# A convolution with pyramid attention on one core: the last batch's scores moved to the start of their steps, six output banks, x of second tiles in halves, and one low part made by VectorE

## The chip, the cores and the metric

The program runs on one NeuronCore of a Trainium2 chip. The metric is the device time of a whole execution in microseconds (us), the median of several runs. Before the change it is 1314.9 us, the median of 3 runs (1314.38 to 1315.77).

The engines named below: PE (TensorE, the matmuls), DVE (VectorE), ACT (ScalarE), POOL (GpSimd) and SP (SyncE, which issues nearly all DMAs). SBUF is the memory on the core, PSUM the eight banks of 128 x 512 numbers that the matmuls write.

## The reference

The input `x` has 8 images of 512 channels with 64 x 64 points. What is computed for each image:

```python
qk = relu(bn(conv1x1(x, qk_w)))            # 256 channels
val = relu(bn(conv1x1(x, v_w)))            # 512 channels
key = psp(qk)                              # max over 1, 9, 36 and 64 windows: 110 cells
value = psp(val).transpose(0, 2, 1)        # 110 cells
query = qk.reshape(B, Ck, H * W).transpose(0, 2, 1)
scores = softmax(einsum('bnc,bcs->bns', query, key) * Ck ** (-0.5))
y = einsum('bns,bsc->bnc', scores, value).transpose(0, 2, 1).reshape(B, Cv, H, W)
return x + bn(conv1x1(y, out_w))
```

All is float32. Keys and values of an image are known only when the whole image has been convolved, so the attention of an image is worked on while the next one is convolved.

## The kernel before, in words

An image is cut into 8 tiles of 512 points; there are 64 tiles (`S`). Every float32 operand of a matmul is split into a high part (`xh`, `wh`, ..: a copy in the fp32r format) and a low part (`xl`, `wl`, ..: the number less its high part), and each product is made of three matmuls of 128 x 128 by 128 x 512 (high x high, low weights x high, high x low), which add up in a PSUM bank. ACT makes the high parts of x, POOL the low parts.

The order of the instructions on each engine is written out by hand; engines wait for each other by counting semaphores. There are three stages.

- Steps 0 and 1 convolve a tile each with plain products. Then come 27 **pairs** (`s` = 1 to 27) of two tiles each. A pair uses a scheme with 7 products in place of 8 (`pair_product`, three times a pair: j = 0, 1, 2; each product part is 6 matmuls, so a j has 42). It needs 7 parts of x (`PARTS`): four blocks of the raw x of the two tiles (B11, B21 of the first, B12, B22 of the second; in `xa`) and three sums of them (`tt[0]` to `tt[2]`, and T3, which overwrites B12), made by POOL in `sums_of_x` (4 instructions). ACT makes the high part of each (`split_part_hi`, L964), then POOL the low part (`split_part_lo`, L578), in the order 0 to 6. With j = 0 PE takes the parts in the same order and waits for the low part of each (`x_ready`). Between its products PE does the attention of tiles 8 behind (`scores`, `sums`, `project`), from pair 4 on.
- DVE pools: row maxima of each product's bank (`pool_pair_rows(s, j, r)`, L1336), cells from the rows (`pool_cells`), and at an image's end the grids. It also adds `u5` in two places (`make_u4` L1399, `make_u7` L1405; PE waits for both), and does steps of the softmax and the final add. In pair 4, 8, 12, .. an image has ended (`batch_ended`), and DVE makes the key cells and grids ahead of `make_u4`.
- SP loads x for pair s + 1 during the lows of pair s: tile 2s + 2 once parts 0 to 3 are split, tile 2s + 3 once part 5 is (`load`, two DMAs of 512 KB each).
- **Steps** 56 to 63 (`LAST` to `S` - 1) convolve the queries' and keys' channels of the last image, tile by tile; steps 64 to 71 (`S` to `X` - 1) load x again and convolve its value channels (`conv(s, 0..3)`, 12 matmuls each), with the softmax of the last image's tiles 56 to 62 beside it: `sums(a)` (2 matmuls) of the tile before at the start of a step, `scores(a)` (6 matmuls) in its middle. The chain for a tile a is: scores on PE, `exps` on ACT (two instructions), `split_e_lo` on DVE, `sums` on PE, `guess` on ACT (two), `refine` (two) and `normalise` on DVE, `split_p_hi` on ACT, `split_p_lo` on DVE; after that `project(a, m)` may run. The queries of tile a are split by `split_q_hi` (ACT) and `split_q_lo` (POOL).
- The **tail**: when the last value cells are there, PE projects all eight tiles 56 to 63 of the last image (`project(a, m)`, m = 0 to 3, 3 matmuls each, 96 in all, and the `sums` of tiles 62 and 63 among them). The output banks are four in turn (`out_bank`), one for each m. DVE adds m = 0, 2, 3 to x (`add_out`, L1476), ACT copies m = 1 out of its bank (`copy_out`, L1235) and POOL adds it (`add_copy`, L608); SP stores each half tile of 512 KB.

## Time and profile before

| | us |
|---|---|
| median of 3 runs | 1314.9 (1314.38 to 1315.77) |
| the profiled execution | 1314.11 |
| its span in the profile | 1312.4 |
| PE busy in the span | 1283.3 (98%) |
| DVE busy | 947.3 (72%) |
| ACT busy | 688.7 (52%) |
| POOL busy | 951.9 (73%) |

The span is what the trace covers; the profiled execution took 1.7 us more than that. A time is read as a start in us from the span's start, then a duration. Where PE is busy 98% of the span, its few idle microseconds are what a change of order can win, and they are in two places: up to about 170 us, and after 1272 us.

### The profile page before, as it was taken

To read this page: it belongs to the slowest core of one execution; us is meant where nothing else is said; L and a number is where in the kernel's file an instruction comes from. 1 tells how busy PE (TensorE), PEld (TensorE's weight loads), DVE (VectorE), ACT (ScalarE), POOL (GpSimd) and SP (SyncE) were. 2 spreads that over 40 slices of the span, in tenths; PEclk is the share of its full clock that TensorE was granted. 3 is DMA by queue.
4 is the path that set the end of the run, shared out by engine and by line. 5 is a ranking of instruction groups with operands and counts; after the bars stand their busy time and mean duration, and the time that the engine had idled before them with its cause. 6 is when DMAs were issued, how large, how long until landed. Compare 5 with 4: busy or idle time off the path is not lost.

```text
span 1312.4 us, 16789 instructions
## 1 busy us (share of the span) xinstructions
PE 1283.3 (98%) x5539; PEld 1036.1 (79%) x5539; DVE 947.3 (72%) x2171; ACT 688.7 (52%) x1017; POOL 951.9 (73%) x414
## 2 busy tenths in 40 slices
PE   7999999999999999999999999999999999999996
PEld 6777788887888878887888877888788887888875
DVE  6555677777777778778777777777867778876466
ACT  5333555644555654555654465654555647754421
POOL 1888988877878867887777786877778826765522
PEclk9999999999999999999999999999999999999998
DMA  6323356566676656676556676666667669995226
GB/s 225 113 97 113 112 177 213 196 217 223 210 240 217 198 187 232 211 238 224 182 207 232 222 232 204 205 200 233 206 219 239 211 205 365 331 308 201 96 97 257
DMA packets 134538, 272.20 MB, mean 207 GB/s; under 512 B 9227, under 2 KB 9267, under 8 KB 134451
## 3 DMA queue, kind: packets, MB, share of 16 engines
q1 hardware_dynamic: 133874, 270.07, 60.9%
q10 hardware_dynamic: 576, 1.05, 0.2%
q8 instruction: 45, 0.74, 0.2%
q14 instruction: 43, 0.34, 0.1%
HBM read 174.61 MB, written 96.47 MB: 207 GB/s over the span
## 4 chain that ended last, share of the span: by engine, by line
PE 79%; DVE 7%; POOL 7%; ACT 3%; DMA 2%; issue 2%; SPq 0%; DVEq 0%; ACTq 0%; POOLq 0%
PE conv_ps L690 16%; PE conv_ps L688 16%; PE conv_ps L692 16%; POOL xl L578 5%; PE out_ps L772 4%; PE out_ps L773 3%; PE out_ps L774 3%; PE conv_ps L673 3%; PE conv_ps L674 3%; PE conv_ps L672 3%; PE score_ps L746 2%; PE score_ps L745 2%; PE score_ps L747 2%; DVE row_max L1336 1%; DMA xa<-x 1%
## 5 line engine op out<-in xcount | busy, mean ns | idle before, releaser
L1336 DVE TENSOR_REDUCE row_max<-conv_ps 128x64 f32<-128x384 f32 (+2 forms) x576 | 284.5, 530 | 149.0 <-ACT q_out L1035 68.2
L578 POOL TENSOR_TENSOR xl<-xa,xh 128x1024 fp32r<-128x1024 f32 x108 | 258.0, 2418 | 84.5 <-ACT xh L964 84.5
L688 PE MATMUL conv_ps<-xh,sh 128*128 128x512 f32 x648 | 253.5, 391 | 3.8 <-POOL xl L578 1.8
L690 PE MATMUL conv_ps<-xh,sl 128*128 128x512 f32 x648 | 254.3, 393 | 0.0
L692 PE MATMUL conv_ps<-xl,sh 128*128 128x512 f32 x648 | 254.3, 392 | 0.0
L578 POOL TENSOR_TENSOR xl<-tt,xh 128x1024 fp32r<-128x1024 f32 x81 | 194.3, 2415 | 10.2 <-ACT xh L964 10.2
L688 PE MATMUL conv_ps<-xh,wh 128*128 128x512 f32 x486 | 190.2, 391 | 4.1 <-POOL xl L578 2.7
L692 PE MATMUL conv_ps<-xl,wh 128*128 128x512 f32 x486 | 190.7, 392 | 0.0
L690 PE MATMUL conv_ps<-xh,wl 128*128 128x512 f32 x486 | 190.6, 392 | 0.0
L972 ACT ACTIVATE conv_ps<-conv_ps 128x512 f32<-128x512 f32 x81 | 47.2, 583 | 253.6 <-PE conv_ps L692 252.9
L1476 DVE SCALAR_TENSOR_TENSOR xo<-out_ps,shift,xo 128x512 f32<-128x512 f32 x205 | 151.9, 745 | 34.5 <-DMA xo<-x 18.0
L602 POOL TENSOR_TENSOR q_l<-q_in,q_h 128x1024 fp32r<-128x1024 f32 x50 | 120.7, 2415 | 47.5 <-ACT q_h L1041 47.5
L688 PEld LDWEIGHTS conv_ps<-xh,sh 128*128 128x128 f32 x648 | 121.7, 188 | 35.7 <-POOL xl L578 4.2
L690 PEld LDWEIGHTS conv_ps<-xh,sl 128*128 128x128 f32 x648 | 121.6, 188 | 28.0
L692 PEld LDWEIGHTS conv_ps<-xl,sh 128*128 128x128 f32 x648 | 121.6, 188 | 26.1
L572 POOL TENSOR_TENSOR xl<-xa,xh 128x1024 fp32r<-128x1024 f32 x34 | 81.4, 2405 | 58.6 <-ACT xh L949 58.6
L589 POOL TENSOR_TENSOR tt<-xa 128x1024 f32<-128x1024 f32 x27 | 64.9, 2405 | 78.0 <-DMA xa<-x 78.0
L688 PEld LDWEIGHTS conv_ps<-xh,wh 128*128 128x128 f32 x486 | 91.3, 188 | 29.2 <-POOL xl L578 4.4
L964 ACT ACTIVATE xh<-xa 128x1024 fp32r<-128x1024 f32 x108 | 113.5, 1055 | 1.4
L690 PEld LDWEIGHTS conv_ps<-xh,wl 128*128 128x128 f32 x486 | 91.2, 188 | 20.6
L692 PEld LDWEIGHTS conv_ps<-xl,wh 128*128 128x128 f32 x486 | 91.2, 188 | 19.4
L672 PE MATMUL conv_ps<-xh,wh 128*128 128x512 f32 x240 | 94.9, 395 | 0.0
(227 smaller groups left out, 2527.7 us busy)
## 6 DMA issues: line engine op xcount, KB each, us to landing
xa<-x SPq DMA_DIRECT2D x148, 512.0 KB, 5.5
xo<-x SPq DMA_DIRECT2D x104, 512.0 KB, 4.3
out<-xo SPq DMA_DIRECT2D x104, 512.0 KB, 3.7
queries<-q_out SPq DMA_DIRECT2D x112, 256.0 KB, 2.5
...
```

What stands on the lines that cost most here:

```text
L572: nc.gpsimd.tensor_tensor(xl[:, b:b + 2, :], xa[:, part, s % 2, :, :], xh[:, b:b + 2, :], ALU.subtract)\
L578: nc.gpsimd.tensor_tensor(xl[:, b0:b1, :], raw, xh[:, b0:b1, :], ALU.subtract).then_inc(x_lo, 1)
L589: nc.gpsimd.tensor_tensor(T1, B12, B11, ALU.subtract).then_inc(t_made, 1)
L602: nc.gpsimd.tensor_tensor(q_l[:, :, :], q_from(a), q_h[:, :, :], ALU.subtract).then_inc(q_lo, 1)
L672: nc.tensor.matmul(bank(s, c)[:, :], wh[:, k, cols], hi, start=(k == 0), stop=False)
L688: nc.tensor.matmul(out[:, :], hi[:, k, :], xh[:, b + k, :], start=first, stop=False, skip_group_check=True)
L690: nc.tensor.matmul(out[:, :], lo[:, k, :], xh[:, b + k, :], start=False, stop=False, skip_group_check=True)
L692: last = nc.tensor.matmul(out[:, :], hi[:, k, :], xl[:, b + k, :], start=False, stop=end, skip_group_check=True)
L772: nc.tensor.matmul(bk[:, :], vo_h[:, cols], hi, start=True, stop=False)
L964: nc.scalar.activation(xh[:, b0:b1, :], raw, ACT.Copy).then_inc(x_hi, 1)
L1336: last = nc.vector.tensor_reduce(row_max[:, c, n, :], src[:, r0_ * W:r1_ * W].rearrange("p (r w) -> p w r", w=W), AX.X, ALU.max)
L1476: nc.vector.scalar_tensor_tensor(xt, out_bank(a, m)[:, :], shift[:, CC + m:CC + m + 1], xt, ALU.add, ALU.add)\
```

## The change

Four edits of order and none of arithmetic:

1. In pairs 2 to 4 (`BY_VECTOR`) the low part of part 5 (B22, `VECTOR_PART`) is made by DVE and no more by POOL. It stands in DVE's program between the third and the fourth row pooling of the pair before with j = 2. Who waited for `x_lo` now waits for `x_lo` and, where needed, `x_lo_vector` (`wait_lo`).
2. SP loads B12 of the second tile of the next pair after part 4 and B22 after part 5; before, both after part 5. POOL's first sum waits for the first half alone (`wait_x_half`).
3. In steps 65 to 70 `scores(a)` stands at the start of the step and `sums(a)` of the same tile in its middle (before: `sums` of the tile before at the start, `scores` in the middle), so that tile 62's softmax ends in step 70 and leaves the tail. ACT, DVE and POOL have their parts of the chain moved to match.
4. The tail turns through six banks (`LAST_BANKS`) and waits for the add (or the copy) of the block six before; `project(56, m)` for m = 1 to 3 waits for no add. `sums(63)` follows tile 57's blocks, not tile 58's.

```diff
@@ parts
+        BY_VECTOR, VECTOR_PART = (2, 3, 4), 5
+        def wait_lo(eng, s, n):
+            v = vector_parts(s)
+            if s in BY_VECTOR and n > VECTOR_PART:
+                v += 1
+            wait(eng, x_lo_vector, v)
+            eng.wait_ge(x_lo, x_parts(s) + n - v)
...
+        LAST_BANKS = [out_ps[0], *conv_ps[0:3], out_ps[1], score_ps]
         def out_bank(a, m):
-            return [out_ps[0], *conv_ps[0:3]][m] if a >= LAST else out_ps[m % 2]
+            return LAST_BANKS[(OC * (a - LAST) + m) % len(LAST_BANKS)] if a >= LAST else out_ps[m % 2]
@@ sync
-                sp.wait_ge(x_lo, x_parts(s) + 6)
-                load(2 * s + 3)
+                wait_lo(sp, s, 5)
+                load_half(2 * s + 3, 0)
+                wait_lo(sp, s, 6)
+                load_half(2 * s + 3, 1)
@@ gpsimd
-                for t in range(2):
-                    wait_x(pool, 2 * s + t)
+                wait_x(pool, 2 * s)
+                wait_x_half(pool, 2 * s + 1, 0)
                 nc.gpsimd.tensor_tensor(T1, B12, B11, ALU.subtract).then_inc(t_made, 1)
                 pool.wait_ge(t_made, 4 * (s - 1) + 1)
+                wait_x_half(pool, 2 * s + 1, 1)
...
                 for i in range(OPS):
-                    split_part_lo(s, i)
+                    if not by_vector(s, i):
+                        split_part_lo(s, i)
...
-                if LAST < s < S:
+                if s < X - 1 and s not in (LAST, S):
                     split_q_lo(s - (NT - 1))
@@ tensor: project
+                n = OC * (a - LAST) + m
+                if n >= len(LAST_BANKS):
+                    n -= len(LAST_BANKS)
+                    if copied(LAST + n // OC, n % OC):
+                        pe.wait_ge(y_copied, n // OC + 1)
+                    else:
+                        pe.wait_ge(out_added, added(LAST + n // OC, n % OC))
...
@@ tensor: steps 64 to 71
-                if s < X - 1:
+                if s <= S + 1:
                     sums(ap)
...
+                elif s < X - 1:
+                    scores(ac)
                 conv(s, 0)
                 conv(s, 1)
...
                 elif s < X - 1:
-                    scores(ac)
+                    sums(ac)
                 conv(s, 2)
...
-            sums(S - 2)
...
-                if a == LAST + 2:
+                if a == LAST + 1:
                     sums(S - 1)
@@ scalar: steps 65 to 70
+            for s in range(S + 1, X - 1):
+                a = s - NT
+                if s == S + 1:
+                    guess(a - 1)
+                exps(a)
+                split_q_hi(a + 1)
+                split_hi(s + 1, 0)
+                split_hi(s + 1, 1)
+                if s == S + 1:
+                    split_p_hi(a - 1)
+                guess(a)
+                split_p_hi(a)
@@ vector
+            def split_vector_part_lo(s):
+                raw, b0, b1 = PARTS[VECTOR_PART]
+                dve.wait_ge(x_hi, part_number(s, VECTOR_PART))
+                nc.vector.tensor_tensor(xl[:, b0:b1, :], raw, xh[:, b0:b1, :], ALU.subtract).then_inc(x_lo_vector, 1)
...
                 pool_pair_rows(s, 2, 2)
+                if s + 1 in BY_VECTOR:
+                    split_vector_part_lo(s + 1)
                 pool_pair_rows(s, 2, 3)
...
             split_e_lo(S - 1)
-            refine(S - 2)
             add_outs(LAST + 1)
-            normalise(S - 2)
             add_outs(LAST + 2)
-            split_p_lo(S - 2)
+            refine(S - 1)
             add_outs(LAST + 3)
-            refine(S - 1)
             normalise(S - 1)
```

The order on DVE from behind `make_u7` of pair 3, j = 2, to `make_u4` of pair 4, before (a row maximum is `row_max`, `make_u4` is L1399; `cells`, `part` and `rows` are the key cells and grids of the image that has ended):

```order
L1336 TENSOR_REDUCE row_max<-conv_ps 128x64 x4
L1379 TENSOR_REDUCE cells<-row_max 128x2x8
L1384 TENSOR_REDUCE part<-row_max 128x2x2 x6
L1377 TENSOR_REDUCE cells<-row_max 128x2x8
L1384 TENSOR_REDUCE part<-row_max 128x2x2 x3
L1419 TENSOR_REDUCE cells<-part 128x2x36
L1421 TENSOR_REDUCE rows<-cells 128x36
L1423 TENSOR_REDUCE cells<-rows 128x2x9
L1425 TENSOR_REDUCE cells<-cells 128x2
L1399 TENSOR_TENSOR conv_ps<-conv_ps,u 128x512
```

and with the change (the same operations have the lines 1397, 1460, 1438 to 1445 and 1480 to 1486):

```order
L1397 TENSOR_REDUCE row_max<-conv_ps 128x64 x2
L1511 TENSOR_TENSOR xl<-xa,xh 128x1024
L1397 TENSOR_REDUCE row_max<-conv_ps 128x64 x2
L1440 TENSOR_REDUCE cells<-row_max 128x2x8
L1445 TENSOR_REDUCE part<-row_max 128x2x2 x6
L1438 TENSOR_REDUCE cells<-row_max 128x2x8
L1445 TENSOR_REDUCE part<-row_max 128x2x2 x3
L1480 TENSOR_REDUCE cells<-part 128x2x36
L1482 TENSOR_REDUCE rows<-cells 128x36
L1484 TENSOR_REDUCE cells<-rows 128x2x9
L1486 TENSOR_REDUCE cells<-cells 128x2
L1460 TENSOR_TENSOR conv_ps<-conv_ps,u 128x512
```

The new subtraction `xl<-xa,xh` stands ahead of the last two row maxima, and so ahead of the chain of cells and grids that ends in `make_u4`.

The order on PE in the tail, tiles 56 and 57 (`e_h`, `sh`: exponentials of the tiles, `vo`: the projected values; three rows are one block), before:

```order
L772 MATMUL out_ps0<-sh,vo_h 128x512 [waits rows_pooled,out_added,vo_lo,p_lo]
...
L772 MATMUL conv_ps0<-sh,vo_h 128x512 [waits out_added,rows_pooled,vo_lo]
...
L772 MATMUL conv_ps1<-sh,vo_h 128x512 [waits out_added,rows_pooled,vo_lo]
...
L772 MATMUL conv_ps2<-sh,vo_h 128x512 [waits out_added,rows_pooled,vo_lo]
...
L772 MATMUL out_ps0<-e_h,vo_h 128x512 [waits out_added,p_lo]
...
L772 MATMUL conv_ps0<-e_h,vo_h 128x512 [waits y_copied]
```

and with the change:

```order
L826 MATMUL out_ps0<-sh,vo_h 128x512 [waits rows_pooled,out_added,vo_lo,p_lo]
...
L826 MATMUL conv_ps0<-sh,vo_h 128x512 [waits rows_pooled,vo_lo]
...
L826 MATMUL conv_ps1<-sh,vo_h 128x512 [waits rows_pooled,vo_lo]
...
L826 MATMUL conv_ps2<-sh,vo_h 128x512 [waits rows_pooled,vo_lo]
...
L826 MATMUL out_ps1<-e_h,vo_h 128x512 [waits p_lo]
...
L826 MATMUL score_ps<-e_h,vo_h 128x512 [waits p_lo]
```

The fifth and the sixth block go to `out_ps1` and `score_ps` and wait for no add; the waits for an add in the first tile are gone but for one at its first block.

The order on PE at the start of step 65, before: the two `sums` of tile 56, then the first rows of `conv(65, 0)`.

```order
L755 MATMUL sum_ps<-sh,ones 128x512 [waits rsum_ready,e_lo]
L756 MATMUL sum_ps<-sl,ones 128x512
L672 MATMUL conv_ps2<-xh,wh 128x512 [waits x_lo,rows_pooled]
L673 MATMUL conv_ps2<-xh,wl 128x512
L674 MATMUL conv_ps2<-xl,wh 128x512
```

With the change, the `scores` of tile 57 stand between them:

```order
L798 MATMUL sum_ps<-sh,ones 128x512 [waits rsum_ready,e_lo]
L799 MATMUL sum_ps<-sl,ones 128x512
L788 MATMUL conv_ps3<-q_h,key_h 128x512 [waits p_lo,q_lo]
L789 MATMUL conv_ps3<-q_h,key_l 128x512
L790 MATMUL conv_ps3<-q_l,key_h 128x512
L788 MATMUL conv_ps3<-q_h,key_h 128x512
L789 MATMUL conv_ps3<-q_h,key_l 128x512
L790 MATMUL conv_ps3<-q_l,key_h 128x512
L715 MATMUL conv_ps2<-xh,wh 128x512 [waits x_lo,x_lo_vector,rows_pooled]
```

They wait for `q_lo`, which POOL makes at the end of step 64.

## Rows read from the trace of the kernel before

**Rows 1.** Windows: us; busy of PE, PEld, DVE, ACT, POOL; PE clock; DMA; GB/s.

```profile
42.00:170.00 128.00, 121.56 (x518) 95.80 (x517) 73.94 (x185) 53.78 (x80) 110.36 (x48) 1.00 0.33 111
...
1272.00:1312.40 40.40, 27.91 (x106) 20.17 (x104) 24.73 (x41) 9.82 (x16) 8.97 (x7) 0.90 0.56 208
```

**Rows 2.** Timeline of PE, pairs 2 to 4: start, duration, [idle before <- releaser].

```profile
86.14 0.39 PE L688 MATMUL conv_ps<-xh,sh 128*128 128x512 f32 x1
...
87.27 0.39 PE L692 MATMUL conv_ps<-xl,sh 128*128 128x512 f32 x1
88.24 0.50 PE L688 MATMUL conv_ps<-xh,sh 128*128 128x512 f32 x1 [0.58 <-POOL xl L578]
...
90.57 0.50 PE L688 MATMUL conv_ps<-xh,wh 128*128 128x512 f32 x1 [0.66 <-POOL xl L578]
...
121.67 0.50 PE L688 MATMUL conv_ps<-xh,wh 128*128 128x512 f32 x1 [0.68 <-POOL xl L578]
...
148.81 0.47 PE L688 MATMUL conv_ps<-xh,sh 128*128 128x512 f32 x1 [0.64 <-DVE conv_ps L1399]
...
152.46 0.50 PE L688 MATMUL conv_ps<-xh,wh 128*128 128x512 f32 x1 [0.65 <-POOL xl L578]
```

**Rows 3.** Timeline of POOL, low parts 3 to 5 of pairs 2 and 4; first sum of pair 3.

```profile
81.08 7.10 POOL L578 TENSOR_TENSOR xl<-xa,xh 128x1024 fp32r<-128x1024 f32 x3
...
95.42 2.40 POOL L589 TENSOR_TENSOR tt<-xa 128x1024 f32<-128x1024 f32 x1 [4.90 <-DMA xa<-x]
...
142.95 7.12 POOL L578 TENSOR_TENSOR xl<-xa,xh 128x1024 fp32r<-128x1024 f32 x3
```

**Rows 4.** Timeline of DVE, ends of pairs 1 and 3.

```profile
81.17 0.69 DVE L1336 TENSOR_REDUCE row_max<-conv_ps 128x64 f32<-128x512 f32 x1 [0.83 <-ACT q_out L1035]
...
144.56 0.82 DVE L1336 TENSOR_REDUCE row_max<-conv_ps 128x64 f32<-128x384 f32 x2 [0.83 <-ACT q_out L1035]
...
147.96 0.70 DVE L1399 TENSOR_TENSOR conv_ps<-conv_ps,u 128x512 f32<-128x512 f32 x1
```

**Rows 5.** Timeline: POOL and DVE at 160 us.

```profile
159.29 2.40 POOL L591 TENSOR_TENSOR tt<-xa,tt 128x1024 f32<-128x1024 f32 x1
161.65 2.79 POOL L592 TENSOR_TENSOR xa<-xa 128x1024 f32<-128x1024 f32 x1
...
160.24 1.93 DVE L1438 TENSOR_TENSOR value_l<-cells,value_h 128x440 fp32r<-128x440 f32 x1
```

**Rows 6.** By source line: count, shortest/median/longest in ns.

```profile
L1438 DVE TENSOR_TENSOR value_l<-cells,value_h x7: 606/608/1929, 160.2 to 1090.8; 128x440 fp32r<-128x440 f32 x7
L1433 DVE TENSOR_TENSOR key_l<-key_d,key_h x8: 378/1536/2407, 154.8 to 1173.2; 128x220 fp32r<-128x220 f32 x8
L1282 DVE TENSOR_TENSOR xl<-xa,xh x2: 1225/1226/1226, 7.0 to 9.8; 128x1024 fp32r<-128x1024 f32 x2
```

**Rows 7.** Timeline, step 64 to 65: PE and POOL.

```profile
1181.49 0.39 PE L756 MATMUL sum_ps<-sl,ones 128*128 128x512 f32 x1
...
1179.55 2.40 POOL L602 TENSOR_TENSOR q_l<-spare_h,q_h 128x1024 fp32r<-128x1024 f32 x1 [2.98 <-ACT q_h L1041]
```

**Rows 8.** Timeline of PE in the tail.

```profile
1274.77 0.47 PE L772 MATMUL out_ps<-sh,vo_h 128*128 128x512 f32 x1 [0.59 <-issue]
...
1286.17 0.50 PE L772 MATMUL conv_ps<-e_h,vo_h 128*128 128x512 f32 x1 [2.10 <-ACT row_max L1235]
...
1297.34 0.40 PE L773 MATMUL out_ps<-sh,vo_l 128*128 128x512 f32 x1
...
1305.30 0.40 PE L774 MATMUL conv_ps<-sl,vo_h 128*128 128x512 f32 x1
```

**Rows 9.** Timeline of DVE and windows (columns as in group 1), tail.

```profile
1304.36 2.15 DVE L1476 SCALAR_TENSOR_TENSOR xa<-conv_ps,shift,xa 128x512 f32<-128x512 f32 x3
...
1287.50:1290.00 2.50, 2.50 (x7) 1.95 (x6) 1.24 (x2) 0.36 (x1) 1.32 (x2) 0.50 0.55 210
...
1307.50:1310.00 2.50, 0.00 (x0) 0.00 (x0) 0.00 (x0) 0.00 (x0) 0.00 (x0) 0.55 1.03 381
```

More of the change, by code:

```diff
@@ L138, in psp_attention @@
         out_ps = [psum(f"out_ps{i}") for i in range(2)]
-        x_in = [sem(f"x_in{i}") for i in range(2)]
+        x_in = sem("x_in")
+        x_in_odd = [sem(f"x_in_odd{i}") for i in range(2)]
         xo_in = [sem(f"xo_in{i}") for i in range(4)]
@@ L281, in pair_banks, with vector_parts, by_vector @@
             return conv_ps[0], conv_ps[2 - n % 2], conv_ps[1 + n % 2], conv_ps[3]
+        BY_VECTOR, VECTOR_PART = (2, 3, 4), 5
+        def vector_parts(s):
+            return len([p for p in BY_VECTOR if p < min(s, PAIRS)])
+        def by_vector(s, i):
+            return s in BY_VECTOR and i == VECTOR_PART
         def part_number(s, i):
@@ L420, in tile_of, with load_half @@
                 return v[i // NT, :, :, i % NT * TN:(i % NT + 1) * TN]
+            def load_half(s, i):
+                sp.dma_start(xa[:, i, s % 2, :, :], tile_of(x_v, tile_at(s))[:, 2 * i:2 * i + 2, :])\
+                    .then_inc(x_in_odd[i] if s % 2 else x_in, 16)
             def load(s):
-                for i in range(2):
-                    sp.dma_start(xa[:, i, s % 2, :, :], tile_of(x_v, tile_at(s))[:, 2 * i:2 * i + 2, :])\
-                        .then_inc(x_in[s % 2], 16)
+                load_half(s, 0)
+                load_half(s, 1)
             def load_residual(h):
@@ L541, in _ @@
                     for a in (LAST + 5, LAST + 7):
-                        sp.wait_ge(x_lo, x_parts(X) - (2 if a == LAST + 5 else 0))
+                        wait_lo(sp, X, -2 if a == LAST + 5 else 0)
                         load_residuals(a)
@@ L634, in _ @@
                         split_lo(n, 1)
-                if s < X - 1 and not LAST < s < S:
+                if s in (LAST, S):
                     split_q_lo(s - (NT - 1))
@@ L938, in split_hi @@
                 if s == 0:
-                    act.wait_ge([x_first, x_in[0]][part], 16)
+                    act.wait_ge([x_first, x_in][part], 16)
                 else:
@@ L1184, in _ @@
                 store_pair_q(s, 3)
-            for s in range(LAST, X):
+            for s in range(LAST, S + 1):
                 ap, ac = s - NT - 1, s - NT
-                if 0 <= ap < S - 2:
-                    guess(ap)
+                guess(ap)
                 if s == LAST + 1:
@@ L1222, in _ @@
                     continue
-                if 0 <= ac < S - 1 and not LAST < s < S:
+                if s == S:
                     exps(ac)
-                if 0 <= ac + 1 < S and not LAST < s < S:
                     split_q_hi(ac + 1)
@@ L1668, in _ @@
                 for c in range(VC):
+                    if c == 2 and S < s < X - 1:
+                        refine(ac)
+                        normalise(ac)
                     pool_tile_rows(s, c)
+                    if c == 2 and S < s < X - 1:
+                        split_p_lo(ac)
                     if s == X - 1:
@@ L1676, in _ @@
                         add_out(ap, 2 * c - 1)
-                    if c == 2 and s < X - 1:
+                    if c == 2 and s == S:
                         split_e_lo(ac)
```

52 lines of the change are left out of this document (31 added, 21 removed).

## The prediction, as put on record before the kernel was run

> **What bounds the kernel now.** I read the page's busy shares first. PE is busy 1283.3 us of 1312.4, so a change of order can win only from the 29.1 us in which PE idles, or from matmuls at a lower clock. The windows by stage come next: 42 to 170 us hold 6.4 us of PE idleness (128.00 less 121.56), and from 1272 us to the end 12.5 us (40.40 less 27.91) [rows 1]; most of the rest lies in the setup before 42 us, which the change leaves alone. In the stretch between, PE has work, so that a wait removed or added on DVE, ACT or POOL costs nothing there unless PE meets it. Third, PE's timeline, where each stop names its releaser: in pairs 2 and 3 it stops twice each for a low part from POOL, in pair 4 once for `make_u4` on DVE and once for POOL [rows 2]. In the tail it stops for adds and for a copy [rows 8].
>
> A stop costs more than its idle time. From 87.27 to 88.24 us two matmuls start 0.97 apart where the usual distance is 0.23 (86.14 and 87.27 are five apart), so an idle time of 0.58 costs 0.74 [rows 2]. I add 0.16 to each idle time.
>
> **Part 1: DVE makes a low part in pairs 2 to 4.** Without anything else it looks like this. POOL makes seven low parts back to back, one each 2.36 us: 81.08 is part 3, and three take 7.10 [rows 3]. PE catches up with part 5 (88.24) and part 6 (90.57). If DVE makes part 5, part 6 is ready 2.36 sooner, and both stops go: 0.74 + 0.82 in pair 2, and 0.84 twice in pair 3 (both its stops have idle 0.68, of which one row stands) [rows 2]. The same subtraction takes DVE 1.23 us in the setup, where POOL is idle [rows 6].
>
> But in the pairs POOL isn't idle, and the trace shows what such an instruction meets. At 160.24 us DVE starts `value_l<-cells,value_h`, with two inputs in SBUF, while POOL is in a subtraction that began at 159.29. The DVE instruction takes 1.93 in place of 0.61, and ends at 162.17; POOL's next one, started at 161.65, takes 2.79 in place of 2.40 [rows 5, 6]. So DVE waited until POOL's instruction was over, then ran, and POOL's next waited for it. `key_l<-key_d,key_h` shows the same: 0.38 at best, 2.41 at worst, never more than one POOL instruction of wait [rows 6]. The new subtraction has two inputs in SBUF as well (`xa`, `xh`).
>
> The Trainium skill states this as a rule, in "SBUF — State Buffer", section "Who interferes with whom": a DVE instruction with two SBUF inputs contends with a GpSimd instruction that reads SBUF, and the one that comes later blocks for the whole instruction. By that rule the new part is no free gain; the trace agrees, with 1.93 against 0.61.
>
> Now the sum with the lock. In pair 2 DVE is free after the third row pooling at 81.86 (81.17 + 0.69) [rows 4]. POOL is in part 3 until 83.44 (81.08 + 2.36). So DVE waits 1.58, runs until 84.67, and the record should show some 2.8 us. POOL's part 4 ends later by nearly DVE's time: at 161.7 DVE ran 0.48 (161.69 to 162.17) and POOL's next took 0.39 longer, 0.1 less than that [rows 5], so 1.23 - 0.1 = 1.13. Part 4 then ends at 86.93 in place of 85.80. PE wanted it at 86.14 [rows 2] and stops 0.8 to 0.85, with the 0.16 a cost of 0.95. After that part 5 is long there, and part 6 (89.3) is ready before PE, now at 89.8 or later. Pair 2: 0.95 in place of 1.56, a gain of 0.6. Pair 3 the same way: 0.95 in place of 1.68, a gain of 0.7.
>
> Pair 4 goes the other way. DVE is free at 143.73 (144.56 less the idle 0.83), POOL's part 3 lasts until 145.31 (142.95 + 2.36), DVE's new instruction until 146.54, and the last row maxima start at 146.55, not at 144.56 [rows 3, 4]. What follows on DVE up to `make_u4` is a chain without a gap (144.56 to 147.96: maxima, cells, grids), so `make_u4` is 2.0 us later, and it is what PE stops for at 148.81 [rows 2, 4]. This stop grows from 0.80 to 2.8. The stop for part 6 (0.81) goes, as PE comes later. Net a loss of 1.2. In pairs 2 and 3 `make_u4` doesn't suffer: DVE is done with the maxima around 85.4, and PE is at part 4 until then waiting for POOL anyway.
>
> Part 1 in all: -0.6 - 0.7 + 1.2 = -0.1, with bounds -3.6 (no lock: -1.56 - 1.68, in pair 4 -0.8 and +0.4 for 1.23 us of DVE in place of a 0.83 gap) and +1.5 (each of DVE's waits a full 2.4).
>
> **Part 2: x in halves.** The first sum of pair 3 waits 4.90 for the DMA [rows 3]. With the halves the load of B12 goes out after part 4 (86.9, against 88.2) and the sum no longer waits for the second half, 512 KB or 1.4 us at the 381 GB/s of [rows 9]: the sum starts about 2.5 us sooner. Nothing on PE waits for that sum now: POOL's low part 0 starts when ACT's high part 0 is there, and that follows PE. Cost and gain nothing from pair 5 on; in pairs 3 and 4 it is what lets POOL keep up with a PE that comes 0.6 to 1.3 sooner, so I give it no term of its own. SP's other loads and stores stand behind the same wait as before.
>
> **Part 3: scores at the step's start.** The matmuls are the same, 56 in a step. What must hold is that q's low part is ready when the step begins. At the first such step it isn't quite: POOL ends it at 1181.95 (1179.55 + 2.40), while PE would start tile 57's scores at 1181.72 (1181.49 + 0.23) [rows 7]. One stop of 0.3 with the 0.16 on top: +0.4, bounds 0 and 1. In later steps q's low part is made in the first half of the step before. POOL has 7.2 us of work in a step of 12.8 us, DVE some 8; ACT comes to x's high parts after exp, copy and q (2.3 us behind the scores), and the low parts then end about 11 us into the step, 1.8 us before the next step asks for them at the earliest. No term.
>
> **Part 4: the tail.** PE's first block starts at 1274.77, behind the value projection, which the change leaves where it is. From there to the last matmul at 1305.30 there are 98 matmuls [rows 8]. Without a stop one follows another at 0.234 (1297.34 to 1305.30 are 34 distances), so the last would start at 1274.77 + 0.08 (the first takes 0.47, not 0.39) + 97 x 0.234 = 1297.55, 7.75 sooner. That includes matmuls at half clock: in 1287.5 to 1290 the granted clock is 0.50, the 1.2 GHz level, behind the stop of 2.10 before 1286.17 [rows 8, 9]; without stops PE should stay at 2.4 GHz.
>
> Is PE free of stops? With six banks a block waits for the add six blocks (4.2 us) back. I walked DVE's new list: 25 adds at 0.70 (three took 2.15 [rows 9]), and five softmax instructions of tile 63, 3.1 together: 20.6 us from the first output at 1275.8, so DVE would be done at 1296.4 if it never waited for PE. Its lag behind PE is greatest at tile 59 (the two `refine` stand before its adds), about 1.4 us, and six banks cover 4.2. Tile 63's own chain ends (low part) near 1291.2, and PE wants it at 1294.9. What four banks and tile 62's `refine`, `normalise` and low part cost is gone. What is late next is the store. The DMA queues move 381 GB/s at the end [rows 9]: 1.05 MB of a tile in 2.75, and PE makes a tile in 12 x 0.234 = 2.81. So the stores just keep up, and the 5.9 us from the last add (1306.51) to the end stay. Tail: -7.7, bounds -7.8 and -4.5 (DMA at 330 GB/s over the eight tiles would give back 3).
>
> **Sum.** -0.1 + 0.4 - 7.7 = -7.4. The profiled execution took 1314.11, 1.7 more than its span, and would take 1306.7; the median of the runs is 0.8 above it, so I say 1307.5.
>
> **The rivals.**
> A, no lock: DVE slips in between, the new instruction takes 1.23, and part 1 gives -3.6. For it: the setup row with 1.23. Against it: 1.93 and 2.41 under the same conditions. 1314.9 - 3.6 + 0.4 - 7.7 = 1304.0.
> B, the tail is handed to the next limit: stores fall behind or DVE's lag reaches the banks, and PE stops again, about 3 us given back. For it: the DMA's share is 1.03 at the end already [rows 9]. That gives 1307.5 + 3 = 1310.5.
> C, the tail gives little, some 2 us in place of 7.7, and the time is 1313: the adds were the limit, and six banks only move the stop. Against it: DVE's 20.6 us of work under PE's 22.8.
> D, slower: POOL in steps 65 to 70 has q's low part first, and x's low parts end after the next step's first matmuls want them. The margin is 1.8 us in 12.8. A step late by 3 us in all would stop PE six times at 1.2 to 2 us; from 1.25 a step on the tail's gain is eaten, at 2.0 a step the time is 1314.9 + 12 - 7.4 = 1319.5. Against it: the walk under part 3, which finds 11 us for a chain that may take 12.8.
> That the change doesn't do what it says, I exclude: the order shows every moved instruction.
>
> **Chances.** Forecast 0.60, A 0.15, B 0.15, C 0.06, D 0.04. A difference under 0.2% (2.6 us) can't be told from none. Faster: the forecast, A, B, 0.91 with a little of C; same 0.05; slower 0.04. The forecast alone reaches from 1306 to 1309; with A and most of B the range is 1303.6 to 1310.6.
>
> **What would show it.** DVE's three new subtractions at about 2.8 us each (right) or 1.2 (A); POOL's part 4 in pairs 2 to 4 at 3.5 in place of 2.4; one stop of PE in pairs 2 and 3, at part 4, and one of about 2.6 idle in pair 4 behind `make_u4`; a stop of 0.3 before tile 57's scores; no stop of PE in the tail and no clock under 1.0 before its last matmul, which starts 7 to 8 us sooner than before, 30.5 less 7.7 = 22.8 us behind the first. Wrong would be new stops at the starts of steps 66 to 71 (D), or `out_ps` and `conv_ps` blocks of the tail waiting for DVE (B, C).

## The result, and the profile after

| | before | after |
|---|---|---|
| median | 1315.13 (1314.38 to 1315.77, 4 runs) | 1306.38 (1304.19 to 1307.34, 4 runs) |
| profiled execution / span | 1314.11 / 1312.4 | 1305.49 / 1303.8 |
| PE busy | 1283.3 | 1280.0 |
| DVE busy | 947.3 | 959.3 |

The ratio is 0.9932 (95% interval 0.9916 to 0.9948, that is 6.8 to 11.0 us less). The forecast was 1307.5, its range 1303.6 to 1310.6.

The two stretches where PE idled, beside [rows 1]; columns as there.

```profile
42.00:170.00 128.00, 121.14 (x515) 96.73 (x514) 83.94 (x187) 53.76 (x80) 106.42 (x44) 0.99 0.34 115
1270.00:1303.80 33.80, 26.81 (x114) 20.76 (x112) 23.77 (x46) 8.12 (x13) 9.09 (x7) 0.98 0.67 249
1275.00:1297.50 22.50, 22.50 (x97) 18.21 (x98) 19.45 (x32) 7.03 (x11) 9.09 (x7) 1.00 0.76 283
```

The tail's 22.5 us are full, at a granted clock of 1.00. The pairs are not better: PE's busy time there is 121.14 where it was 121.56, DVE's is up by 10 us (73.94 to 83.94), and the clock reads 0.99.

**The tail.** PE's timeline of the changed kernel: the end of the value projection and the first block, and the last matmul.

```profile
1273.46 0.39 PE L843 MATMUL out_ps<-woT_h,value_l 128*128 128x512 f32 x1
1274.91 0.47 PE L826 MATMUL out_ps<-sh,vo_h 128*128 128x512 f32 x1 [1.06 <-issue]
...
1297.57 0.40 PE L828 MATMUL conv_ps<-sl,vo_h 128*128 128x512 f32 x1
```

From first to last it is 22.66 us, without a stop, where it was 30.53 [rows 8]: 7.87 less. Two of the stops that are gone stood in tile 56, the tail's first. There the kernel before let block m wait for the add of the block ahead, although each had a bank of its own (PE before):

```profile
1276.72 0.47 PE L772 MATMUL conv_ps<-sh,vo_h 128*128 128x512 f32 x1 [0.31 <-DVE xo L1476]
...
1278.67 0.47 PE L772 MATMUL conv_ps<-sh,vo_h 128*128 128x512 f32 x1 [1.01 <-DVE xo L1476]
```

The longest stop, 2.10 before 1286.17 [rows 8], waits for ACT's copy, and the copy stands in ACT's program behind tile 62's high part, which waited 7.76 us for the last step of that tile's softmax on DVE (ACT before):

```profile
1284.95 0.60 ACT L1095 ACTIVATE sh<-score_ps 128x512 fp32r<-128x512 f32 x1 [7.76 <-DVE score_ps L1459]
1285.44 0.68 ACT L1235 ACTIVATE row_max<-conv_ps,shift 128x512 f32<-128x512 f32 x1
```

**Pairs 2 and 4.** The same view: where pair 2 had two stops [rows 2], there is one, at part 4. Pair 4's stop behind `make_u4` is 2.46, and the matmuls behind it start some 0.42 apart in place of 0.23. The last row is the window of that piece, with the clock at 0.50, the 1.2 GHz level.

```profile
85.61 0.39 PE L735 MATMUL conv_ps<-xl,wh 128*128 128x512 f32 x1
86.61 0.50 PE L731 MATMUL conv_ps<-xh,sh 128*128 128x512 f32 x1 [0.61 <-POOL xl L616]
...
145.20 0.39 PE L735 MATMUL conv_ps<-xl,wh 128*128 128x512 f32 x1
148.05 0.47 PE L731 MATMUL conv_ps<-xh,sh 128*128 128x512 f32 x1 [2.46 <-DVE conv_ps L1460]
...
150.06 0.63 PE L731 MATMUL conv_ps<-xh,sh 128*128 128x512 f32 x1
150.48 0.63 PE L733 MATMUL conv_ps<-xh,sl 128*128 128x512 f32 x1
```
```profile
149.70:152.20 2.50, 2.50 (x8) 1.92 (x7) 1.52 (x3) 0.00 (x0) 2.50 (x2) 0.50 0.52 188
```

DVE's new instruction over the whole program, by line, and its timeline and POOL's in pair 2 (before: [rows 3, 4]):

```profile
L1511 DVE TENSOR_TENSOR xl<-xa,xh x3: 2665/2790/2790, 81.5 to 141.1; 128x1024 fp32r<-128x1024 f32 x3
```
```profile
81.52 2.79 DVE L1511 TENSOR_TENSOR xl<-xa,xh 128x1024 fp32r<-128x1024 f32 x1
84.23 0.81 DVE L1397 TENSOR_REDUCE row_max<-conv_ps 128x64 f32<-128x384 f32 x2
```
```profile
80.81 5.75 POOL L616 TENSOR_TENSOR xl<-xa,xh 128x1024 fp32r<-128x1024 f32 x2
```

POOL's two parts take 5.75 where three took 7.10 [rows 3], two thus 4.73: part 4 is 1.0 longer, with DVE's turn in it.

**Pair 1, which I had not looked at.** The halves bring POOL's first sum of pair 2 from 63.42 to 58.70, and there it meets DVE's split of the weight combinations, `sl`, which also has two SBUF inputs. DVE before, then DVE, POOL and PE after:

```profile
61.24 1.22 DVE L1311 TENSOR_TENSOR sl<-s_raw,sh 128x1024 fp32r<-128x1024 f32 x1
62.37 1.22 DVE L1311 TENSOR_TENSOR sl<-q_in,sh 128x1024 fp32r<-128x1024 f32 x1
```
```profile
60.21 1.95 DVE L1372 TENSOR_TENSOR sl<-s_raw,sh 128x1024 fp32r<-128x1024 f32 x1
62.09 3.41 DVE L1372 TENSOR_TENSOR sl<-q_in,sh 128x1024 fp32r<-128x1024 f32 x1
```
```profile
58.70 2.39 POOL L627 TENSOR_TENSOR tt<-xa 128x1024 f32<-128x1024 f32 x1 [0.98 <-DMA xa<-x]
61.16 3.25 POOL L630 TENSOR_TENSOR tt<-xa,tt 128x1024 f32<-128x1024 f32 x1
64.38 3.37 POOL L631 TENSOR_TENSOR xa<-xa 128x1024 f32<-128x1024 f32 x1
```
```profile
62.22 0.50 PE L731 MATMUL conv_ps<-xh,sh 128*128 128x512 f32 x1 [1.43 <-DVE sl L1372]
```

PE's stop for `sl` was 0.68 before. It follows the first of the two records: first records of 1.22, 1.95, 2.13, 2.46 and 3.17 us (before, this trace, and runs 1, 3 and 8 below) have stops of 0.68, 1.43, 1.60, 1.93 and 2.64 behind them. A long second record alone cost nothing at this stop: in run 6, which has no part 2, it is 3.42 and the stop 0.69.

### The profile page after: what moved, and what is told of

Read it like the earlier page. It is cut to its first block, busy times and chain, and to the rows that moved or that the text cites. A ratio compares the mean times of both kernels' runs of the same rounds, so it can differ in the third digit from the quotient of the medians.

```text
span 1303.8 us, 16985 instructions
## 1 busy us (share of the span) xinstructions
PE 1280.0 (98%) x5539; PEld 1036.2 (79%) x5539; DVE 959.3 (74%) x2174; ACT 689.2 (53%) x1017; POOL 949.7 (73%) x411
## 4 chain that ended last, share of the span: by engine, by line
PE 85%; DVE 7%; ACT 3%; POOL 3%; issue 2%; DMA 0%; DVEq 0%; SPq 0%; ACTq 0%
PE conv_ps L733 17%; PE conv_ps L731 17%; PE conv_ps L735 17%; PE out_ps L826 4%; PE out_ps L827 4%; PE conv_ps L716 4%; PE conv_ps L715 4%; PE conv_ps L717 4%; PE out_ps L828 4%; POOL xl L616 3%; PE score_ps L789 2%; PE score_ps L788 2%; PE score_ps L790 2%; DVE row_max L1397 1%; ACT xh L1019 1%
## 5 line engine op out<-in xcount | busy, mean ns | idle before, releaser
L616 POOL TENSOR_TENSOR xl<-xa,xh 128x1024 fp32r<-128x1024 f32 x105 | 253.8, 2437 | 95.7 <-ACT xh L1019 95.7
L610 POOL TENSOR_TENSOR xl<-xa,xh 128x1024 fp32r<-128x1024 f32 x34 | 81.1, 2405 | 35.0 <-ACT xh L1004 35.0
```

The costliest lines, as they stand in the source:

```text
L610: nc.gpsimd.tensor_tensor(xl[:, b:b + 2, :], xa[:, part, s % 2, :, :], xh[:, b:b + 2, :], ALU.subtract)\
L616: nc.gpsimd.tensor_tensor(xl[:, b0:b1, :], raw, xh[:, b0:b1, :], ALU.subtract).then_inc(x_lo, 1)
```

## The experiments

The kernel before was timed beside each group of runs on the same chip (medians 1313.97 to 1315.07), so ratios carry the comparison; a median is set beside another only where the two ran together. Intervals of the ratios are about 0.0013 to each side (1.7 us). "Extra" below is start to start less the usual distance, idle time plus 0.16.

Effects of 1 us are small against such intervals, but PE runs the same matmuls in the same order through the pairs, so each profiled execution can be held against the trace of before at the same matmul. The table has how much later (+) or sooner (-) than before three matmuls start, those at 60.07, 85.00 and 170.01 us in the trace of before: the first number is the difference that is there at 60 us, the others are what is added to it in the stretch with pair 1's `sl` and in pairs 2 to 4.

| kernel | at 60 us | 60 to 85 us | 85 to 170 us |
|---|---|---|---|
| changed | -1.03 | +0.74 | +0.13, half clock in pair 4 |
| run 1, the same again | +0.26 | +0.91 | -1.04 |
| run 5, changed up to the tail | -0.16 | +0.91 | -1.10 |
| run 7, no halves | +0.03 | -0.02 | +0.20, half clock |
| run 11, POOL's sum waits for `sl` | +0.60 | 0.00 | +0.19, half clock |
| run 2, no part 1 | -0.80 | -0.02 | -0.11 |
| run 12, no parts 1 and 2 | +1.20 | -0.03 | -0.34 |
| run 6, before with five banks | +0.55 | -0.02 | +1.23 |
| run 3, pairs 2 and 3 | 0.00 | +1.21 | -2.20 |
| run 8, pairs 2 and 3, late load | -0.63 | +3.51 | -2.16 |
| run 9, pairs 2 and 3, sum waits | -0.70 | -0.02 | -2.13 |
| run 10, part 0 | -0.17 | -0.02 | -2.85 |
| run 4, one input from PSUM | +0.13 | +1.12 | -4.76 |

The first column is scatter for the most part: of the change only the load for pair 2 acts before 60 us, and run 12, without that, has the largest number there. Run 6 has the pairs of before and still loses 1.23 in them, to three stops for low parts in pair 4 (0.66, 0.68 and 0.68) where before has two stops in all, and one for `make_u7` (0.49): so a single trace can be off by that much. The three kernels with pairs 2 and 3 agree within 0.07.

**1. The changed kernel once more.** No edit.

> The changed kernel as it is, timed once more as the yardstick of the runs beside it. Both theories: about 1306.4 us, ratio to before 0.993. Its first four times lay 3.1 us apart (1304.19 to 1307.34), those of before 1.4. If the clock's fall behind make_u4 in pair 4 (8 matmuls at half clock, 1.5 us) comes in only some executions, the spread returns and the best times lie near 1305; if it comes always, this profile shows it again at the same place.

Measured: 1306.22 (1305.64 to 1307.03), ratio 0.9933. Pair 4's stop is there again (idle 2.42), but the clock behind it stays at 1.00:

```profile
149.70:152.20 2.50, 2.50 (x12) 2.03 (x13) 1.24 (x3) 1.07 (x4) 2.50 (x2) 1.00 1.03 397
```

So the half clock (1.5 us) comes in some executions. Run 5's trace, which has the same pairs, is the second without it, behind the same idle time of 2.42:

```profile
149.70:152.20 2.50, 2.50 (x13) 2.05 (x12) 1.44 (x3) 0.61 (x2) 2.50 (x2) 1.00 0.95 361
```

In pair 1 `sl` stopped PE for 1.60.

**2. Without part 1.**

```diff
-        BY_VECTOR, VECTOR_PART = (2, 3, 4), 5
+        BY_VECTOR, VECTOR_PART = (), 5
```

> The changed kernel without part 1: POOL makes all seven low parts again. Theory 'lock': DVE's subtraction waits for POOL and POOL for it, so part 1 gives nothing in sum. The changed kernel stops 0.77 in pair 2, 0.81 in pair 3, 2.62 in pair 4 and loses 1.53 at half clock behind that, 5.7 in all; without part 1 the stops should be those of before, 1.56 + 1.68 + 1.6 = 4.8. So this kernel is 0.9 us FASTER than the changed one, about 1305.5. Rival 'DVE's help is worth its cost': this kernel is slower by 3 us or more, 1309.5, as the forecast's case A had it.

Measured: 1306.60 (1305.31 to 1308.56), ratio 0.9936 (0.9923 to 0.9949). The stops of before are back (extras 0.75, 0.85, 0.74, 0.84, 0.80, 0.81). The time is that of the changed kernel within the scatter, and the rival with 3 us is out. The medians can't tell the 0.9 us that I expected. By the table, pairs 2 to 4 add -0.11 here and -0.34 in run 12, against about +0.2 with part 1 where the half clock comes and -1.1 where it doesn't: part 1 loses some 0.4 or gains some 0.9.

**3. DVE's part in pairs 2 and 3 alone.**

```diff
-        BY_VECTOR, VECTOR_PART = (2, 3, 4), 5
+        BY_VECTOR, VECTOR_PART = (2, 3), 5
```

> The changed kernel with DVE's low part in pairs 2 and 3 alone. Theory 'lock, and make_u4 behind it': pairs 2 and 3 keep their single stops of about 0.8 (gain 0.8 each), pair 4 goes back to two stops of about 0.8 and no half clock, so 4.15 - 1.6 = 2.5 us less than the changed kernel, about 1303.9. Rival 'the loss in pair 4 is only moved': what PE gains there it loses again at the next stop (values or scores of tile 0), and the time stays within 0.5 us of 1306.4.

Measured: 1305.18 (1304.35 to 1306.33), ratio 0.9924 (0.9911 to 0.9936), 1.0 below run 1. Pair 4 is back at extras of 0.82 and 0.82, as expected, but PE's stop for `sl` in pair 1 was 1.93 here. By the table the loss in pair 4 is 2.3 where the half clock comes (-2.20 for +0.13; 2.5 was expected) and 1.2 where it doesn't (for -1.04 in run 1), and the rival, that what is gained there is lost again at the next stop, is not borne out up to 170 us. Against runs 2 and 12 the two pairs gain some 1.9.

**4. The same subtraction with one input from PSUM.** The values of that low part are then not x's.

```diff
-                nc.vector.tensor_tensor(xl[:, b0:b1, :], raw, xh[:, b0:b1, :], ALU.subtract).then_inc(x_lo_vector, 1)
+                nc.vector.tensor_tensor(xl[:, b0, :], sum_ps[:, :], xh[:, b0, :], ALU.subtract)
+                nc.vector.tensor_tensor(xl[:, b0 + 1, :], sum_ps[:, :], xh[:, b0 + 1, :], ALU.subtract)\
+                    .then_inc(x_lo_vector, 1)
```

> The changed kernel, but DVE's low part is made by two 512-wide subtractions that take the first input from a PSUM bank in place of x in SBUF (the values of this part are then not x's low part; size, place and waits are the same). Theory 'lock': with one SBUF input nothing is shared with POOL, so each takes some 0.6 to 0.7 us in the record with no wait in it, 1.3 in sum in place of 2.8, and POOL's part 4 takes 2.4 in place of 3.5. The stops of pairs 2 and 3 (0.77, 0.81) go, that of make_u4 in pair 4 falls from 2.46 idle to about 1.3, and the half clock behind it goes: 1.6 + 1.3 + 1.5 = some 4.3 us less, about 1302. Rival 'the subtraction is slow in the pairs for another reason (its operands in SBUF are being written, or DMA traffic)': the xh input and the output are still there, the record keeps 2 us or more, and the time stays near 1306.

Measured: 1301.51 (1300.33 to 1303.73, 4 runs), ratio 0.9897 (0.9882 to 0.9913), 4.7 below run 1. DVE and POOL in pair 2, and PE's stop in pair 4:

```profile
83.04 0.68 DVE L1511 TENSOR_TENSOR xl<-sum_ps,xh 128x512 fp32r<-128x512 f32 x1
83.64 0.68 DVE L1512 TENSOR_TENSOR xl<-sum_ps,xh 128x512 fp32r<-128x512 f32 x1
```
```profile
82.34 4.75 POOL L616 TENSOR_TENSOR xl<-xa,xh 128x1024 fp32r<-128x1024 f32 x2
```
```profile
146.33 0.47 PE L731 MATMUL conv_ps<-xh,sh 128*128 128x512 f32 x1 [0.91 <-DVE conv_ps L1460]
```

POOL was in an instruction when DVE started, and DVE did not wait (0.68, 0.68); nor did POOL (4.75 for two). No low part stops PE in pairs 2 and 3. The output and one SBUF input are still there, so it is the second SBUF input that makes DVE wait for POOL. The edit also cuts the instruction in two; that a shorter one would not wait is spoken against by `value_l`, 440 columns with two SBUF inputs, which took 1.93 in place of 0.61 [rows 5, 6], though no run cut it with both inputs in SBUF. The run shows what the lock takes from part 1: 3.0 us by the stops (extras of 0.73, 0.79 and 2.58 in run 1, of 1.07 alone here), 3.7 by the table, 4.7 by the medians.

**5. Four output banks in the tail.**

```diff
-        LAST_BANKS = [out_ps[0], *conv_ps[0:3], out_ps[1], score_ps]
+        LAST_BANKS = [out_ps[0], *conv_ps[0:3]]
```

(The one wait that only the sixth bank needs, `n == 5`, goes with it. Tile 56's blocks wait for no add, as in the changed kernel.)

> The changed kernel with four output banks in the tail, as before, in place of six; tile 62's softmax stays where the change puts it. Theory 'chain' (what the tail gained is that refine, normalise and the low part of tile 62 left DVE, and its guess and high part left ACT): DVE's adds take 2.1 of every 2.8 us, so four banks (2.8 us back) cover it except where tile 63's refine and normalise stand before adds; the tail grows by 0 to 1.5 us, about 1307.2. Theory 'banks': four banks bring back most of the 7.7 us, with the 2.1 us stop and the half clock behind it, about 1312.

Measured: 1306.49 (1306.37 to 1306.72), ratio 0.9943 (0.9930 to 0.9955). In the whole tail there is one stop:

```profile
1286.73 0.47 PE L823 MATMUL out_ps<-sh,vo_h 128*128 128x512 f32 x1 [0.17 <-DVE spare_h L1539]
```

First to last matmul: 1274.73 to 1297.81, 23.08 us. The fifth and sixth bank are worth 0.4 of the tail's 7.9.

**6. The kernel before with five banks**, tile 62's softmax still in the tail (the sixth bank holds its scores).

```diff
-            return [out_ps[0], *conv_ps[0:3]][m] if a >= LAST else out_ps[m % 2]
+            return LAST_BANKS[(OC * (a - LAST) + m) % 5] if a >= LAST else out_ps[m % 2]
+        LAST_BANKS = [out_ps[0], *conv_ps[0:3], out_ps[1]]
```

(The waits for the adds are counted five blocks back, and tile 56's blocks 1 to 3 wait for none, as in the changed kernel.)

> The kernel before with five output banks in the tail (the sixth, score_ps, still holds tile 62's scores there), everything else as before, tile 62's softmax in the tail too. Theory 'banks': one bank more takes half or more of the stops away, 4 us sooner than before, 1311. Theory 'chain': DVE and ACT have tile 62's and 63's chains between the adds, and PE waits for tile 62's low part or for a copy whatever the banks; 0 to 2 us sooner, about 1314.

Measured: 1311.65 (1310.09 to 1313.58, 11 runs), ratio 0.9979 (0.9970 to 0.9988), some 2.5 us. First to last matmul 27.28 (1276.77 to 1304.05): the stops for adds went, this one stayed, with the half clock behind it:

```profile
1286.40 0.50 PE L781 MATMUL out_ps<-e_h,vo_h 128*128 128x512 f32 x1 [2.16 <-ACT row_max L1244]
...
1287.77 0.63 PE L783 MATMUL conv_ps<-e_l,vo_h 128*128 128x512 f32 x1
```

The profiled execution is the slowest of the 11 (1313.58). Run 6 takes 3.3 off the tail, run 5 7.5, the whole change 7.9. Both runs also have the waits of tile 56 out, and these alone were worth an estimated 1.65, the two stops of before with 0.16 for each (0.31 + 1.01 + 0.32). So without them the fifth bank is worth about 1.6, the removed chain about 5.8 and both 6.2. No run took the waits of tile 56 out alone. The stop of 2.1 goes only with the chain.

**7. Without the halves.** `load(2 * s + 3)` whole behind low part 6, and POOL's first sum waits for both.

```diff
-                wait_lo(sp, s, 5)
-                load_half(2 * s + 3, 0)
                 wait_lo(sp, s, 6)
-                load_half(2 * s + 3, 1)
+                load(2 * s + 3)
```

> The changed kernel without part 2: both halves of a pair's second tile are loaded behind low part 6, and POOL's first sum waits for both. What the prediction says: nothing on PE waits for that sum, so the pairs keep their times, T1 of pair 3 starts some 2.5 us later (95 in place of 92.4). What the trace of the changed kernel adds: in pair 1 the sooner sum meets DVE's sl, both take a wait, and PE stops 1.58 in place of 0.84. So 0.7 us sooner by pair 2, about 1305.7. Rival 'the halves carry part 1': POOL, late by 2.5 us, is late with the sums or low part 0 of the next pair, and the kernel is 1 to 3 us slower, 1308.

Measured: 1306.22 (1305.65 to 1306.91), ratio 0.9941 (0.9928 to 0.9953). `sl` takes 1.21 and 1.22, PE's stop for it is 0.69; the other stops are those of the changed kernel, the half clock in pair 4 included. So part 1 needs no halves, and the rival is out. The 0.7 us are not to be told in the median, but they are in the table: -0.02 in place of +0.74 in pair 1, and the same in pairs 2 to 4 (+0.20, +0.13). POOL's first sum of pair 3 starts at 92.72, not at the 95 that I expected.

**8. Pairs 2 and 3 alone, and the first half of the load in pair 1 issued behind low part 6 with the second.** POOL's first sum still waits for the first half alone.

```diff
-                wait_lo(sp, s, 5)
+                wait_lo(sp, s, 5 if s > 1 else 6)
```

> DVE's low part in pairs 2 and 3 alone, and the halves from the load for pair 3 on (the load of pair 2's second tile goes out whole behind low part 6, as before). If the collision of POOL's first sum of pair 2 with DVE's sl costs the 0.74 us that the trace of the changed kernel shows, this is 0.7 us under the kernel with pairs 2 and 3 and all halves, about 1303.2. If the collision only moves to another instruction, the two are equal within 0.3.

Measured: 1306.52 (1304.19 to 1307.15), ratio 0.9939 (0.9927 to 0.9951). The expectation failed: the meeting is still there, and worse. DVE and POOL in pair 1:

```profile
60.61 3.17 DVE L1372 TENSOR_TENSOR sl<-s_raw,sh 128x1024 fp32r<-128x1024 f32 x1
63.70 3.39 DVE L1372 TENSOR_TENSOR sl<-q_in,sh 128x1024 fp32r<-128x1024 f32 x1
```
```profile
60.34 2.35 POOL L627 TENSOR_TENSOR tt<-xa 128x1024 f32<-128x1024 f32 x1 [2.22 <-DMA xa<-x]
62.77 3.24 POOL L630 TENSOR_TENSOR tt<-xa,tt 128x1024 f32<-128x1024 f32 x1
```

The edit moved the load but left POOL's wait for the first half alone, so it took only one of part 2's two sides away. In the six traces with all of part 2 and no wait for `sl` POOL's first sum starts at 58.12 to 60.26, here at 60.34, and in the four where it waits for both halves (before, runs 6, 7 and 12) at 62.41 to 63.67. Within each group the DMA decides, and so whether the sum meets `sl`. PE stopped for 2.64 here, the clock was 0.57 in the 4 us behind it, and pair 1 cost 3.51 by the table.

**9. Pairs 2 and 3, and POOL's first sum of pair 2 waits for `sl`.** To run 3 it adds:

```diff
+                if s == 2:
+                    pool.wait_ge(s_lo, 3)
                 nc.gpsimd.tensor_tensor(T1, B12, B11, ALU.subtract).then_inc(t_made, 1)
```

> DVE's low part in pairs 2 and 3 alone, halves as in the changed kernel, and POOL's first sum of pair 2 waits until DVE has made sl's last part, so the two no longer overlap. The profiles so far show the meeting as a matter of when the DMA brings x: with it PE's stop behind sl costs 1.6 to 2.8 us (idle 1.43, 1.60, 1.93, 2.64), without it 0.84. Theory 'collision': this profile has that stop at 0.84 and sl's two records at 1.22 us each; the median is 1 to 1.5 us under the kernel with pairs 2 and 3 alone (1305.2), about 1304, and the five times lie closer together than 2 us. Rival 'POOL needed the head start': the sums and low parts of pair 2 end later, the stops in pair 2 grow by what pair 1 gains, time 1305 to 1306.

Measured: 1303.33 (1302.41 to 1304.09, 4 runs), ratio 0.9910 (0.9897 to 0.9924). `sl` takes 1.22 twice, PE's stop is 0.67, and POOL, 5.01 idle, is not missed (the stops of pairs 2 to 4 are those of run 3). Against run 3's 0.9924 the intervals overlap, so the size of the gain is the traces' word, not the medians': 1.2 us in pair 1 (-0.02 for +1.21), and nothing lost in pairs 2 to 4.

**10. DVE makes low part 0 in place of 5**, in pairs 2 to 4, right before `make_u4` of the pair ahead, with the wait of run 9.

```diff
-        BY_VECTOR, VECTOR_PART = (2, 3, 4), 5
+        BY_VECTOR, VECTOR_PART = (2, 3, 4), 0
...
+                if s + 1 in BY_VECTOR:
+                    split_vector_part_lo(s + 1)
                 make_u4(s, 2)
```

> As the run before, but DVE makes low part 0 in place of 5, in pairs 2 to 4, right before make_u4 of the pair ahead, when POOL idles behind ACT's high part 0 (2.94 us of idle before 105.03). Theory 'lock': with POOL idle DVE's subtraction takes 1.23 us, nobody waits, and POOL starts part 1 when ACT's high part 1 is there, 1.1 us sooner than now. The stops before parts 5 and 6 shrink from 0.75 and 0.84 to one of some 0.4 in all in each of pairs 2 to 4, DVE's make_u4 of the pair ahead comes 0.3 later and meets no wait of PE: 1.3 us less than with part 5 in pairs 2 and 3, about 1302.7. Rival: ACT, not POOL, paces the series (POOL waits for every high part), so that the sooner start is lost by part 2 and the stops stay at 0.8 each, about 1305.5. Second rival: the u4 of the pair ahead is now late and PE stops there for 0.5 to 1 us in each, 1306.

Measured: 1302.83 (1302.22 to 1303.22, 4 runs), ratio 0.9906 (0.9893 to 0.9920), the fastest of those that leave nothing out, though not clear of run 9 (1303.33); by the table its pairs 2 to 4 gain 0.7 more. DVE's instruction by line, POOL's first part in pair 3, and PE's one stop there:

```profile
L1513 DVE TENSOR_TENSOR xl<-xa,xh x3: 1214/1216/1218, 74.0 to 133.8; 128x1024 fp32r<-128x1024 f32 x3
```
```profile
105.15 4.77 POOL L616 TENSOR_TENSOR xl<-tt,xh 128x1024 fp32r<-128x1024 f32 x2 [5.45 <-ACT xh L1021]
```
```profile
119.44 0.47 PE L733 MATMUL conv_ps<-xh,wh 128*128 128x512 f32 x1 [0.68 <-issue]
```

The same instruction that took 2.79 takes 1.22 where POOL idles. Pairs 2 and 3 keep one stop of 0.84, not the 0.4 that I expected; pair 4 keeps that of `make_u4` (0.80) and loses that of part 6. No `make_u4` came late.

**11. The changed kernel with run 9's wait alone**, DVE's part in pairs 2 to 4.

> The changed kernel with one wait more: POOL's first sum of pair 2 waits until DVE has made sl's last part. It tells pair 1's collision from pair 4's stop: 'collision' says 0.7 to 1.9 us under the changed kernel, 1305 to 1305.5, and pair 4 keeps its stop of 2.4 us idle; against the kernel with pairs 2 and 3 alone and the same wait it should be 1 us slower (pair 4: 2.6 less 1.6), or 2.5 in executions with the half clock behind that stop.

Measured: 1304.74 (1304.48 to 1306.89), ratio 0.9921 (0.9907 to 0.9934). It ran beside run 9 and is 1.4 slower by the median, with intervals that overlap; by the table pairs 2 to 4 lose 2.3 against run 9, half clock included. Its profiled execution is the slowest, 1306.89, and has the half clock behind the stop of 2.45 (it was also 0.60 late at 60 us); the other four lie between 1304.48 and 1304.88, and whether the half clock came in them no trace shows.

**12. Parts 3 and 4 alone.** Runs 2 and 7 in one.

> The changed kernel without parts 1 and 2: the scores half a step sooner, tile 62's chain ahead of the tail and the six banks are all that is left of the change. If the pairs (parts 1 and 2) net nothing and the tail is all of the gain, the terms read from the trace of the changed kernel add up to it: +0.3 (stop before tile 57's scores), +0.5 (two sums matmuls now in the bound stretch), -7.9 (first to last matmul of the tail), -0.9 (last add to end 5.0 in place of 5.9): 8.0 us under before, ratio 0.994, and pairs 1 to 4 with the stops of before. If part 1 had a worth of its own this run is 1 us or more behind the changed kernel; if it is only a burden, 1 us ahead.

Measured: 1307.25 (1305.52 to 1307.75), ratio 0.9943 (0.9930 to 0.9957): 7.5 us of the changed kernel's 8.9 by the ratios, and the two intervals overlap. First to last matmul of the tail: 1275.88 to 1298.55, 22.67. The 0.9 us from the last add to the end isn't here: from the last matmul's start to the end it is 7.15, where before has 7.10 and the changed kernel 6.23. Over the twelve traces with the new tail it is 6.15 to 7.16, and in run 6, with the old one, 7.85. So it scatters by as much as the term, and I should not have put it in this run's sum.

## Why the prediction held, point by point

**Sum.** -7.4 was forecast, 8.8 less was measured (1315.13 to 1306.38); with run 1 8.5 less. The two spans differ by 8.60: -1.03 up to 60 us, +0.74 in pair 1, +0.13 in pairs 2 to 4, -0.52 from 170 us to 1163.90, +0.82 from there to the first block of the tail, -7.87 in the tail, -0.87 behind it. What the change did in this execution is thus -6.2 (0.74 + 0.13 + 0.82 - 7.87), in run 1 by the same reckoning -7.1, and the other -2.4 lie where no part of it acts or where traces differ by as much (run 12). That the forecast came within 1.4 us of the medians is therefore in part luck: its pairs were about 1 us too good for the profiled execution, and 1.4 to 2.6 us of the 8.5 to 8.8 between the medians no term explains.

**Part 1, -0.1: right in the mechanism, near in size.** DVE's records are 2.67 to 2.79 (2.8 forecast), the stops at part 4 cost 0.77 and 0.81 (0.95), pair 4's costs 2.62 (2.8), an idle time of 2.46 (2.6 in the list of signs). POOL's part 4 ends 5.75 behind the start of part 3 (5.85 forecast). Held against the trace of before, pairs 2 to 4 came out at +0.13. In this sum two misses cancel: pairs 2 and 3 gained 2.3 together (1.3 forecast; 0.3 of it is extra waiting that only the trace of before has in pair 3), and pair 4 lost 2.4 with the half clock (1.2 forecast, and 1.2 in run 1 without it). One reason for the first is that a stop costs more than idle time plus 0.16: the matmul behind it takes 0.47 or 0.50, and the next one starts 0.08 or 0.11 later than usual (88.24 to 88.58 in the trace of before). The prediction counts this for the tail's first block and for no other stop. Run 4 shows what the lock withholds. It doesn't bear out the size in case A (no lock, 1304.0): it measured 1301.51, 2.5 less. This case's runs agree with the rule in the Trainium skill, "SBUF — State Buffer", section "Who interferes with whom": 2.79 for 1024 columns with two SBUF inputs beside a busy POOL, 0.68 per 512 columns with one.

**Part 1, what was missed:** the stop of 2.46 pulls the clock to 1.2 GHz behind it, 1.5 us, in three of five profiles that have it (changed, runs 7 and 11; not in runs 1 and 5). I had the same thing before me in the tail of before, a stop of 2.10 with a clock of 0.50 behind [rows 8, 9], used it there, and did not carry it to a stop whose cost I myself forecast at 2.8.

**Part 2, 0: right for pairs 3 and 4, wrong for pair 1, where it cost 0.7 in this trace.** The sum of pair 3 starts 3.1 sooner (92.36 for 95.42; 2.5 forecast), and nothing on PE waits for it. But the halves are not what brought it: without them it starts at 92.72 (run 7), so with part 1 in place, which ends POOL's lows sooner, they bring 0.4 there at most. "Cost and gain nothing" rested on pairs 3 and 4; in pair 1 the sooner sum meets `sl`, at a cost of 0.74 in the trace (run 7 has it at none). I had the lock, and did not ask which other instructions of DVE with two SBUF inputs the moved POOL work would fall on.

**Part 3, +0.4: right.** The changed kernel before tile 57's scores:

```profile
1180.79 0.40 PE L799 MATMUL sum_ps<-sl,ones 128*128 128x512 f32 x1
1181.31 0.50 PE L788 MATMUL conv_ps<-q_h,key_h 128*128 128x512 f32 x1
```

0.52 for 0.23, a cost of 0.29. A term was missed: the two matmuls of tile 62's sums stood in the gap before the tail's first block, where PE waited anyway (PE of before):

```profile
1273.54 0.39 PE L755 MATMUL sum_ps<-sh,ones 128*128 128x512 f32 x1
1273.78 0.40 PE L756 MATMUL sum_ps<-sl,ones 128*128 128x512 f32 x1
1274.77 0.47 PE L772 MATMUL out_ps<-sh,vo_h 128*128 128x512 f32 x1 [0.59 <-issue]
```

Now they stand where PE is full, 0.46 more, and the gap's idle time is 1.06. This is read from the two traces; no run undid it alone.

**Part 4, -7.7: right in size (-7.87), without saying what carries it.** The walk of the tail held: no stop, clock 1.00, 22.8 forecast and 22.66 measured. But I gave the six banks and the removed chain the gain together, and did not name the waits of tile 56, an estimated 1.65 of it. With the chain and these waits gone four banks are nearly enough (23.08, run 5); a fifth bank and these waits gone, with the chain still there, take 3.3 of the 7.9 (run 6). I could have seen it in my own walk: DVE's lag of 1.4 is less than the 2.8 us that four blocks cover.

**Cases B, C and D** did not come: no stop in the tail and no step's start late. C and D are excluded by the first trace, and B too.

What stays open: why the half clock stayed out in runs 1 and 5, behind stops of 2.42, and came in run 7 behind one of 2.41; and why PE's times up to 60 us differ by up to 2.2 us between executions (first column of the table), which is most of what blurs the small terms. The traces of the other executions are not there, so how often the half clock comes is known from five alone.
